# A decoder layer on one core: residual sums of the last batches on TensorE, the down product in another bank, and all orders written anew

## The chip, the cores and the metric

One core of a Trainium2 chip runs the whole kernel. The metric is device time in microseconds (us) of one execution. The core has a matrix engine (TensorE, PE in the profile, with its weight loads as PEld), a vector engine (VectorE, DVE), a scalar engine (ScalarE, ACT), GpSimd (POOL) and SyncE (SP), which here only starts transfers. Each engine runs its own list of instructions in order and waits on semaphores for the others. Matrix products land in PSUM, eight banks of 512 float32 columns by 128 partitions; everything else is in SBUF.

## The reference, cut to what matters

```python
# x: (16, 256, 128), ctx: (16, 64, 128), float32
x = _layernorm(x + attn(x))      # 16 heads of 8, linear attention, elu+1 features, own layernorm with gamma and beta
x = _layernorm(x + xattn(x, ctx))# 16 heads of 64, softmax over 64 context rows
x = _layernorm(x + ffn(x))       # I = 352
def ffn(x):                      # fp4_linear(v, w) = einsum(q(v), q(w)), q: blocks of 16 to 8 levels and back
    return fp4_linear(silu(fp4_linear(x, w_gate)) * fp4_linear(x, w_up), w_down)
```

`q` divides each block of 16 values by its largest magnitude over 6, rounds to a grid of eight magnitudes and multiplies back. All products are in float32 accuracy.

## The kernel before, in words

**Tiling.** A batch has two tiles (t = 0, 1) of 128 rows, so there are 32 tiles. Weights are folded once at the start: `m_product` (32 calls) gives, per head and half of the batches, the matrix `M` with which a tile's 16 x 64 scores come from the normed rows in two products.

**Stages of one batch.** `project_kv`, `project_q`, `kv_outer`, `kv_project`, `attn_out` (linear attention), two norms (`attn`, `post`), `x1_transpose`, then per tile `scores`, `score_max` on DVE, `scores_shift` on PE (the maxima are taken off by a product with an identity), `softmax_exp` on ACT, `fold_halves`, `score_sums`, `score_reciprocals`, `probabilities` (POOL, DVE, DVE, POOL), `p_transpose`, `keep_pT` on ACT, `cross_out`. Then `cross_residual` on DVE, `statistics` and `aggregate` on DVE, four short POOL operations for reciprocal deviation and shift, `cross_norm` on ACT, the quantisation of x2 (DVE, ACT, DVE, DVE, POOL: `x_max` to `x_dequantise`), `xf_transpose`, a split of the result into a high and a low part (`xf_cut_high` and `xf_keep_low` on DVE, `keep_xfT` on ACT), `gate_up` per tile in three float32r products for each of gate and up, `gate_tanh`, `gate_times`, `gated`, the quantisation of h (`h_max` to `h_dequantise`), `h_transpose`, `keep_hT`, `down`, `ffn_residual`, statistics, norm and the store.

**The last batch.** Batch 15 goes tile by tile from `tile_cross_out` on, through functions named `tile_...`, and its gate and up products are whole float32 products (L2912 to L2916). Both of its down products land in bank A2.

**Banks.** A1 (attention sums and small values), A2 (projections, `cross_out`, `xf_transpose`, and `down`, by `DN = A2`), S (two banks, scores), TP (two banks, TP0 and TP1: `p_transpose`, `values`, `h_transpose`), F (two banks, F0 and F1: gate and up products, then the magnitudes in the quantisation of h; batch 13 uses S for them). A product into a bank waits until the readers of what was there are done. That wait stands in the list ahead of the call.

**Orders.** The calls of a batch are not in a loop: each engine's list is written out, some 430 calls on POOL, 540 on ACT, 725 on DVE and 400 on PE, so that up to nine batches are under way at once. `keep_warm(bank, n)` issues n products of a 128 x 128 identity (each is two entries in the profile) into a bank, with no reader. It is called three times: `WARM` = 8 at the very start into A1, 7 ahead of `h_transpose(13)` and 14 ahead of `h_transpose(14)`, both into TP0.

The ends of PE's list before, waits left out: ... `p_transpose(15, 1)`, `xf_transpose(14)`, `tile_cross_out(15, 1)`, `gate_up(14, 0)`, `h_transpose(12)`, `down(12)`, `gate_up(14, 1)`, `keep_warm(TP0, 7)`, `h_transpose(13)`, `tile_xf_transpose(15, 0)`, `tile_gate_up(15, 0)`, `down(13)`, `tile_xf_transpose(15, 1)`, `tile_gate_up(15, 1)`, `keep_warm(TP0, 14)`, `h_transpose(14)`, `down(14)`, `tile_h_transpose(15, 0)`, `tile_h_transpose(15, 1)`, `tile_down(15, 0)`, `tile_down(15, 1)`.

Of the kernel before, what the change touches and what calls it, by code (L numbers as in the profile page):

```python
# [17 lines left out]
def decoder_layer(nc, x, x_t, attn_w, attn_rows, ctx_t, wq_t, wk_t, wv_t, wo_in, fw_in, out):  # L18
# [40 lines left out]
    with es:  # L59
# [57 lines left out]
        NXB, NA, NPE = 4, 5, 3  # L117
# [26 lines left out]
        fold = several("fold", 2, [P, HX * R // 2])  # L144
        ssum = several("ssum", 2, [P, HX])
        srec = several("srec", 2, [P, HX])
# [4 lines left out]
        xf_r = several("xf_r", 2, [P, 2, T * P], FP32R)  # L151
        xfT = sb("xfT", [P, T * P])
# [21 lines left out]
        DN = A2  # L174
# [5 lines left out]
        FFN_IN_S = (13,)  # L180

# [62 lines left out]
        XO_OF, GU_OF = (A2, A1), ((F0, F1), (S0, S1))  # L244

# [32 lines left out]
        WARM = 8  # L278
# [9 lines left out]
        def _(sp):  # L288
# [31 lines left out]
            load_xT(4)  # L320
            load_x(4)
            load_x(5)
            load_xT(5)
            load_xT(6)
            load_x(6)
            load_x(7)
            load_x(8)
            load_xT(7)
            load_xT(8)
            load_xT(9)  # L330
            load_x(9)
            load_x(10)
            load_x(11)
            load_xT(10)
            load_xT(11)
            load_x(12)
            store_out(0)
            store_out(1)
            load_xT(12)
            load_x(13)  # L340
            store_out(2)
            load_x(14)
            load_xT(13)
            load_xT(14)
            store_out(3)
            load_x(15)
            load_xT(15)
            store_out(4)
# [16 lines left out]
        def _(pool):  # L365
# [54 lines left out]
            def fold_halves(b, t):  # L420
                n = T * b + t
                pool.wait_ge(pe_made, n + 1)
                wait_free(pool, ssum_made, n - 1)
                p4 = pe_[n % NPE][:, :].rearrange("p (h s r) -> p h s r", h=HX, s=2)
                ge.tensor_tensor(by_head(fold[n % 2][:, :]), p4[:, :, 0, :], p4[:, :, 1, :], ALU.add).then_inc(fold_made, 1)  # L425

            def probabilities(b, t):
# [3 lines left out]
                ge.tensor_tensor(w, w, spread(srec[n % 2][:, :], HX, R), ALU.mult).then_inc(pn_made, 1)  # L431
# [83 lines left out]
            gate_up_low(0)  # L515
            gate_up_low(1)
# [4 lines left out]
            times_gamma(0)  # L521
            plus_x_beta(0)
            k_norm(1)
# [5 lines left out]
            k_norm(2)  # L529
# [6 lines left out]
            x_plus_rows(3)  # L536
            fold_halves(0, 0)
            minus_mean("post", 1)
            variance_eps("post", 1)
            k_norm(3)  # L540
            rstd_of("post", 1)
            shift_of("post", 1)
            probabilities(0, 0)
            variance_eps("attn", 2)
            fold_halves(0, 1)
# [3 lines left out]
            probabilities(0, 1)  # L549
# [3091 lines left out]
```

## Time and profile before

| what | us |
|---|---|
| median of 3 runs (372.3 to 372.66) | 372.65 |
| the profiled execution's own time | 374.35 |
| its span, first to last instruction | 372.6 |
| PE busy in the span | 351.0 |
| DVE busy | 307.9 |
| POOL busy | 269.1 |
| ACT busy | 253.4 |

The profiled execution took 1.7 us more than the median, and its span is nearly the median. PE's busy time is modelled at its ends and holds the drain of each product, so that it overstates what the array does: a 128-column float32 product is two entries of about 275 ns each, while in a row of sixteen such entries one starts every 111 ns.

### The profile page before, as it was taken

The page shows a single profiled execution, that of the slowest core. Times are in us where ns is not written, and L with a number is a line of the kernel's source. Part 1 is how long each engine was busy: PE and PEld are TensorE (multiplying, and loading weights), DVE is VectorE, ACT ScalarE, POOL GpSimd, SP SyncE. Part 2 cuts the span into 40 slices and gives each one's busy share as a digit, 9 for nine tenths or more (in the row PEclk, how much of TensorE's full clock was granted, in tenths as well). Part 3 has the DMA queues.
Part 4 walks back from the last instruction along what each step waited for, and adds up shares of the span by engine and source line. Part 5 has one row for each costly group of instructions (what it writes and reads, how often), then busy time and mean ns, then how long its engine had stood idle before and what let it go on. Part 6 is the DMA issues. An engine that isn't in the chain of part 4 may idle for free.

```text
span 372.6 us, 7321 instructions
## 1 busy us (share of the span) xinstructions
PE 351.0 (94%) x2143; PEld 268.7 (72%) x2143; DVE 307.9 (83%) x858; ACT 253.4 (68%) x533; POOL 269.1 (72%) x453
## 2 busy tenths in 40 slices
PE   7999998999998999999999999999999999998874
PEld 6688655775775968778678867786777788887663
DVE  2798756658689998869989779979998998999994
ACT  2757867586677678668687767868767656864553
POOL 4403549967988689969779895898989569784535
PEclk9999999999999999999999999999999999999998
DMA  7900100001000001000000000000000000000010
GB/s 251 300 2 16 30 1 14 16 16 29 15 17 14 2 15 43 16 30 17 15 29 14 17 1 17 28 3 0 17 15 2 15 2 0 8 23 14 3 30 28
DMA packets 13586, 10.44 MB, mean 28 GB/s; under 512 B 971, under 2 KB 12396, under 8 KB 13548
## 3 DMA queue, kind: packets, MB, share of 16 engines
q1 hardware_dynamic: 12540, 7.89, 7.0%
q10 hardware_dynamic: 1008, 2.10, 1.7%
q8 instruction: 18, 0.29, 0.3%
q14 instruction: 20, 0.16, 0.1%
HBM read 7.88 MB, written 2.10 MB: 27 GB/s over the span
## 4 chain that ended last, share of the span: by engine, by line
PE 71%; POOL 8%; DVE 8%; issue 6%; ACT 5%; DMA 1%; POOLq 0%; ACTq 0%; DVEq 0%
PE A L2860 13%; PE S L2833 12%; PE TP L2823 7%; PE F L2879 6%; PE TP L2851 6%; PE A L2895 5%; PE A L2784 3%; PE S L2842 3%; PE TP L2762 2%; POOL pe L431 2%; PE S L2762 2%; PE F L2762 2%; PE TP L2888 2%; PE A L2797 2%; DMA wqkT<-in_wk_t 1%
## 5 line engine op out<-in xcount | busy, mean ns | idle before, releaser
L431 POOL TENSOR_TENSOR pe<-pe,srec 128x1024 f32<-128x1024 f32 x32 | 60.9, 1904 | 9.2 <-DVE srec L1835 8.9
L2833 PE MATMUL S<-M,x1T 128*128 128x512 f32 x128 | 60.7, 597 | 1.5 <-ACT pe L1064 1.4
L2860 PEld LDWEIGHTS A<-wvoT,wqkT 128*128 128x128 f32 x480 | 56.4, 192 | 3.1 <-issue 1.8
L2860 PE MATMUL A<-wvoT,wqkT 128*128 128x128 f32 x480 | 58.0, 276 | 0.1
L425 POOL TENSOR_TENSOR fold<-pe 128x512 f32<-128x512 f32 x32 | 40.8, 1276 | 14.5 <-ACT pe L1064 14.2
L1818 DVE TENSOR_REDUCE smax<-S 128x16 fp32r<-128x1024 f32 x32 | 38.7, 1210 | 3.2 <-PE S L2833 3.1
L1064 ACT ACTIVATE pe<-S 128x1024 f32<-128x1024 f32 x32 | 32.6, 1020 | 10.6 <-PE S L2842 10.3
L1069 ACT ACTIVATE wqkT<-TP 128x1024 f32<-128x1024 f32 x32 | 32.6, 1019 | 4.3 <-PE TP L2851 4.1
L2833 PEld LDWEIGHTS S<-M,x1T 128*128 128x128 f32 x128 | 22.2, 190 | 18.3 <-issue 15.3
L2879 PE MATMUL F<-w_gu_r,xf_r 128*128 128x352 f32 x168 | 35.0, 344 | 0.1
L2851 PE MATMUL TP<-ident,pe 128*128 128x128 f32 x256 | 33.5, 274 | 1.6 <-POOL pe L431 1.0
L2851 PEld LDWEIGHTS TP<-ident,pe 128*128 128x128 f32 x256 | 28.8, 140 | 6.2 <-issue 3.1
L2823 PE MATMUL TP<-HW,ctx_f 128*64 128x512 f32 x128 | 31.0, 605 | 0.0
L2879 PEld LDWEIGHTS F<-w_gu_r,xf_r 128*128 128x128 f32 x168 | 26.9, 188 | 4.4 <-issue 3.2
L2895 PEld LDWEIGHTS A<-w_dn,hT 128*128 128x128 f32 x180 | 21.5, 192 | 6.6 <-issue 4.7
L441 POOL TENSOR_TENSOR hv<-hv,ham 128x704 f32<-128x704 f32 x15 | 20.8, 1389 | 6.0 <-DVE hv L1910 5.8
L1829 DVE TENSOR_REDUCE ssum<-fold 128x16 f32<-128x512 f32 x32 | 21.7, 677 | 4.2 <-POOL fold L425 4.2
L416 POOL TENSOR_TENSOR kn<-fk,ky 128x256 f32<-128x256 f32 x16 | 10.1, 632 | 20.7 <-DVE ky L1790 20.6
L2895 PE MATMUL A<-w_dn,hT 128*128 128x128 f32 x180 | 23.0, 277 | 2.0 <-ACT hT L1089 2.0
L2842 PE MATMUL S<-smax,ident_r 128*128 128x512 f32 x64 | 21.8, 422 | 1.7 <-DVE smax L1818 1.7
L409 POOL TENSOR_TENSOR xb<-x_sb,rows 128x512 f32<-128x512 f32 x16 | 20.4, 1275 | 3.9 <-DMA rows<-in_attn_rows 2.7
L1058 ACT ACTIVATE wvoT<-TP 128x1024 f32<-128x1024 f32 x16 | 16.3, 1022 | 6.8 <-PE TP L2823 6.8
(247 smaller groups left out, 890.2 us busy)
## 6 DMA issues: line engine op xcount, KB each, us to landing
xT<-in_x_t SPq DMA_DIRECT2D x16, 128.0 KB, 2.1
x_sb<-in_x SPq DMA_DIRECT2D x16, 128.0 KB, 2.1
out<-yf SPq DMA_DIRECT2D x15, 128.0 KB, 1.8
M<-in_fw SPq DMA_DIRECT2D x1, 560.0 KB, 11.0
wqkT<-in_wq_t ACTq DMA_DIRECT2D x2, 256.0 KB, 4.5
wqkT<-in_wk_t ACTq DMA_DIRECT2D x2, 256.0 KB, 5.8
ctx_f<-in_ctx_t ACTq DMA_DIRECT2D x2, 256.0 KB, 6.9
wvoT<-in_wv_t ACTq DMA_DIRECT2D x1, 512.0 KB, 9.2
```

The lines of the kernel that those rows point to most:

```text
L425: ge.tensor_tensor(by_head(fold[n % 2][:, :]), p4[:, :, 0, :], p4[:, :, 1, :], ALU.add).then_inc(fold_made, 1)
L431: ge.tensor_tensor(w, w, spread(srec[n % 2][:, :], HX, R), ALU.mult).then_inc(pn_made, 1)
L1064: sc.activation(pe_[n % NPE][:, :], S[:, :], ACT.Exp, scale=SCALE).then_inc(pe_made, 1)
L1069: sc.activation(pT[n % 2], TP[:, :].rearrange("p (a n) -> p a n", a=NJ), ACT.Copy).then_inc(pT_kept, 1)
L1818: ve.tensor_reduce(smax[n % 2][:, :], by_head(S[:, :]), AX.X, ALU.max, negate=True).then_inc(smax_made, 1)
L2823: last = te.matmul(TP[par * R:par * R + R, half * BANK:half * BANK + BANK], ctx_f[:, b * R:b * R + R], HW[:, par, 4 * half:4 * half + 4, : ...
L2833: last = te.matmul(S[:, half * BANK:half * BANK + BANK], x1T[b % 2][:, t * P:t * P + P], M[:, b // BH, HC * half:HC * half + HC, b % BH * ...
L2842: last = te.matmul(S[:, half * BANK:half * BANK + BANK], ident_r[:, :], spread(smax[n % 2][:, HC * half:HC * half + HC], HC, R), start=Fal ...
L2851: last = te.transpose(TP[:, j * P:j * P + P], pe_[n % NPE][:, j * P:j * P + P], ident[:, :])
L2860: last = te.matmul(A2[:, t * P:t * P + P], pT[n % 2][:, j, :], vo[b % 2][:, j, :], start=(j == 0), stop=(j == NJ - 1))
L2879: last = te.matmul(bk[:, 0:I], part(xf_r[b % 2][:, left, :], t), w_gu_r[:, right, m, :], start=(n == 0), stop=(n == len(PARTS) - 1))
L2895: last = te.matmul(DN[:, t * P:t * P + P], hT[b % 2][:, t, k * P:k * P + P], w_dn[:, k, :], start=(k == 0), stop=(k == NK - 1))
```

## The change

- Batches 13 and 14: `cross_out` and `down` begin each tile's sum with a product of the identity and the residual (`x1`, `x2`), so that `cross_residual` and `ffn_residual` fall away on DVE; `statistics` and the norm read PSUM. The same for the down product of both tiles of batch 15.
- Batches 12, 13 and 14: `gate_up` makes whole float32 products (two per tile in place of six in float32r). `xf_cut_high` and `xf_keep_low` fall away on DVE, and `keep_xfT` copies from PSUM.
- `down` lands in TP0 (`DN = TP0`). The down product of batch 15's second tile lands in A1, the first one's stays in A2.
- `xf_r` lies in the space of `GT`, `xfT` gets two buffers. `NFO` = 2 only names a number that was there.
- `WARM` goes from 8 to 13, and there are now five calls of `keep_warm`: at the start (13), 3 into F0 ahead of `m_product(0, 0)`, 7 into TP0 ahead of `h_transpose(13)`, 4 into F0 ahead of `tile_gate_up(15, 0)`, 15 into TP0 ahead of `tile_h_transpose(15, 0)`.
- The lists of all five engines are written anew from the first batch to the last.

```diff
-        WARM = 8
+        WARM = 13
-        DN = A2
+        DN = TP0
+        WHOLE_GATE = (12, 13, 14)
+
+        SUM_ON_PE = (13, 14)
+
+        TILE_SUM_ON_PE = True
...
+        DN_OF = (A2, A1) if TILE_SUM_ON_PE else (A2, A2)
...
+                y = part(A2, t) if b in SUM_ON_PE else yx[b % 2][:, t, :]
+                norm("cross", b, t, x2[b % 3][:, NBX * t:NBX * t + NBX, 0:BLK], blocks(y, NBX))
...
             def keep_xfT(b):
-                act.wait_ge(xf_cut_made, b + 1)
-                sc.activation(xf_r[b % 2][:, 0, :], xf_cut[:, :], ACT.Copy).then_inc(xfT_kept, 1)
+                if b in WHOLE_GATE:
+                    act.wait_ge(xfT_made, b + 1)
+                    sc.activation(xfT[b % 2][:, :], A2[:, 0:T * P], ACT.Copy).then_inc(xfT_kept, 1)
...
+                if b in SUM_ON_PE:
+                    pe.wait_ge(x1_made, T * b + T)
+                    te.matmul(part(A2, t), ident[:, :], x1[b % NA][:, t, :], start=True, stop=False)
                 for j in range(NJ):
...
+                if b in WHOLE_GATE:
+                    for m, bk in enumerate(ffn_banks(b)):
+                        last = te.matmul(bk[:, 0:I], part(xfT[b % 2], t), w_gu[:, m, :], start=True, stop=True)
+                    last.then_inc(gu_made, 1)
+                    return
...
             def down(b):
                 pe.wait_ge(hT_kept, b + 1)
                 for t in range(T):
+                    if b in SUM_ON_PE:
+                        pe.wait_ge(x2_made, T * b + T)
+                        te.matmul(blocks(part(DN, t), NBX), ident[:, :], x2[b % 3][:, NBX * t:NBX * t + NBX, 0:BLK],
+                                  start=True, stop=False)
```

The end of PE's list:

```diff
+            pe.wait_ge(hg4_made, 13)
+            gate_up(14, 0)
             pe.wait_ge(xg_made, 15)
             tile_cross_out(15, 1)
...
             pe.wait_ge(h_made, 29)
             gate_up(14, 1)
-            pe.wait_ge(hT_kept, 13)
+            pe.wait_ge(pT_kept, 32)
             keep_warm(TP0, 7)
             h_transpose(13)
...
+            pe.wait_ge(hT_kept, 14)
+            down(13)
+            pe.wait_ge(xfT_kept, 15)
             tile_xf_transpose(15, 0)
-            pe.wait_ge(h_made, 30)
+            pe.wait_ge(hg4_made, 15)
+            keep_warm(F0, 4)
             tile_gate_up(15, 0)
             pe.wait_ge(xfT_kept, 16)
-            down(13)
-            pe.wait_ge(yf_made, 14)
             tile_xf_transpose(15, 1)
+            pe.wait_ge(normed["ffn"], 28)
+            h_transpose(14)
             pe.wait_ge(hg4_made, 14)
             tile_gate_up(15, 1)
-            pe.wait_ge(hT_kept, 14)
-            keep_warm(TP0, 14)
-            h_transpose(14)
+            pe.wait_ge(hT_kept, 15)
+            down(14)
+            pe.wait_ge(normed["ffn"], 30)
+            keep_warm(TP0, 15)
+            tile_h_transpose(15, 0)
+            pe.wait_ge(normed["ffn"], 30)
+            tile_h_transpose(15, 1)
             pe.wait_ge(xfT_kept, 17)
```

`normed["ffn"]` reaches 30 when ACT has done `ffn_norm(14, 1)`; `hg4_made` reaches 15 when DVE has done `h_rounded(14)`.

On the other engines the lists now end so:

- DVE, after `tile_cross_residual(15, 1)`: `gate_times(14, 1)`, `tile_x_reciprocal(15, 0)`, `gated(14, 1)`, `tile_x_scaled(15, 0)`, `h_max(14)`, `h_reciprocal(14)`, `h_scaled(14)`, `tile_statistics("cross", 15, 1)`, `tile_x_rounded_up(15, 0)`, `tile_x_rounded(15, 0)`, `tile_aggregate("cross", 15, 1)`, `h_rounded_up(14)`, `statistics("ffn", 13)`, `aggregate("ffn", 13)`, `h_rounded(14)`, the five steps of the quantisation of x2 for (15, 1), `tile_gate_times(15, 0)`, `tile_gated(15, 0)`, `tile_h_max(15, 0)`, `tile_h_reciprocal(15, 0)`, `tile_h_scaled(15, 0)`, `tile_gate_times(15, 1)`, `tile_h_rounded_up(15, 0)`, `tile_gated(15, 1)`, `statistics("ffn", 14)`, `tile_h_max(15, 1)`, `aggregate("ffn", 14)`, `tile_h_reciprocal(15, 1)`, `tile_h_scaled(15, 1)`, `tile_h_rounded(15, 0)`, `tile_h_rounded_up(15, 1)`, `tile_h_rounded(15, 1)`, then statistics and aggregates of both last tiles.
- ACT: ..., `keep_hT(14)`, `tile_gate_tanh(15, 1)`, `tile_h_magnitudes(15, 0)`, `tile_h_magnitudes(15, 1)`, `ffn_norm(14, 0)`, `ffn_norm(14, 1)`, `tile_keep_hT(15, 0)`, `tile_keep_hT(15, 1)`, `tile_ffn_norm(15, 0)`, `tile_ffn_norm(15, 1)`. Before, `ffn_norm(14, 0)` and `(14, 1)` stood behind both `tile_keep_hT`.
- POOL: ..., four short operations for `"ffn", 14`, `tile_h_dequantise(15, 0)`, `tile_h_dequantise(15, 1)`, the short operations of the last two norms.

## Rows read from the trace of the kernel before

**Rows 1.** Stretches: us, busy time of PE, PEld, DVE, ACT, POOL, granted clock, DMA.
```profile
0.00:10.00 10.00, 7.21 (x36) 6.54 (x37) 3.27 (x15) 2.12 (x3) 4.56 (x24) 1.00 0.80 253
...
50.00:60.00 10.00, 8.32 (x36) 4.98 (x33) 7.17 (x22) 5.91 (x17) 6.91 (x13) 1.00 0.05 14
60.00:300.00 240.00, 234.55 (x1442) 176.74 (x1442) 202.93 (x585) 175.90 (x369) 198.12 (x312) 1.00 0.05 16
...
320.00:344.40 24.40, 22.54 (x155) 19.26 (x154) 23.34 (x58) 15.72 (x29) 15.47 (x25) 1.00 0.06 17
344.40:364.50 20.10, 16.19 (x115) 13.86 (x114) 19.10 (x52) 10.06 (x21) 8.95 (x21) 1.00 0.05 15
```
**Rows 2.** The chain that ended last, a piece: start, us on the chain, what.
```profile
284.48 1.34 PE A L2895 x12
285.81 1.72 PE S L2833 x4
287.75 0.97 PE F L2879 x6
288.72 0.87 PE TP L2851 x8
290.03 1.78 PE A L2860 x16
```
**Rows 3.** The page's costliest groups: busy us, mean ns, idle before.
```profile
L1818 DVE TENSOR_REDUCE smax<-S 128x16 fp32r<-128x1024 f32 x32 | 38.7, 1210 | 3.2 <-PE S L2833 3.1
...
L1064 ACT ACTIVATE pe<-S 128x1024 f32<-128x1024 f32 x32 | 32.6, 1020 | 10.6 <-PE S L2842 10.3
```
**Rows 4.** Two lines of DVE: ns min/median/max, first and last start.
```profile
L1915 DVE TENSOR_TENSOR yf<-A,x x15: 392/425/426, 134.8 to 364.7; 128x256 f32<-128x256 f32 x15
...
L1876 DVE TENSOR_TENSOR xf_r<-A,xf_cut x15: 390/418/426, 103.3 to 343.0; 128x256 fp32r<-128x256 f32 x15
```
**Rows 5.** PE in order of time, the start: start, us, operation.
```profile
1.45 3.78 PE L2934 MATMUL A<-fold 128*128 128x128 f32 x16 [1.45 <-POOL fold L371]
6.57 2.08 PE L2742 MATMUL F<-wqkT 64*128 64x128 f32 x16 [1.34 <-DMA wqkT<-in_wk_t]
...
11.00 1.16 PE L2742 MATMUL TP<-wqkT 64*128 64x128 f32 x16
...
12.97 1.65 PE L2762 MATMUL F<-ctx_r,GT 128*128 128x512 f32 x6
...
16.08 1.66 PE L2762 MATMUL TP<-ctx_r,GT 128*128 128x512 f32 x6
```
**Rows 6.** All engines in order of time, the start.
```profile
14.74 1.28 DVE L1712 TENSOR_TENSOR GT<-TP,pe 128x512 fp32r<-128x512 f32 x2
```
**Rows 7.** PE in order of time, `scores(15, 0)` and `tile_cross_out(15, 1)`.
```profile
319.95 1.88 PE L2833 MATMUL S<-M,x1T 128*128 128x512 f32 x4
...
341.74 2.02 PE L2905 MATMUL A<-wvoT,wqkT 128*128 128x128 f32 x16 [0.49 <-ACT wqkT L1069]
```
**Rows 8.** All engines in order of time, the end: the filler products and their surroundings.
```profile
357.88 3.29 PE L2934 MATMUL TP<-ident 128*128 128x128 f32 x28
...
359.54 0.88 ACT L1036 ACTIVATE yf<-yf,shift_ffn,rstd_ffn 128x128 f32<-128x128 f32 x2 [1.00 <-POOL shift_ffn L462]
...
361.25 0.64 PEld L2888 LDWEIGHTS TP<-ident,hv 128*128 128x128 f32 x6 [0.28 <-POOL hv L441]
```
**Rows 9.** The same view, from the last rounding of h to the last residual sum.
```profile
363.93 0.53 DVE L1997 SCALAR_TENSOR_TENSOR hv<-S,hv 128x352 f32<-128x352 f32 x1
...
364.54 0.79 POOL L508 TENSOR_TENSOR hv<-hv,ham 128x352 f32<-128x352 f32 x1 [0.40 <-DVE hv L1997]
...
365.47 0.52 PE L2922 MATMUL TP<-ident,hv 128*128 128x128 f32 x3 [0.44 <-POOL hv L508]
...
367.04 0.94 PE L2928 MATMUL A<-w_dn,hT 128*128 128x128 f32 x6 [0.38 <-DVE yf L2003]
...
368.01 0.29 DVE L2003 TENSOR_TENSOR yf<-A,x 128x128 f32<-128x128 f32 x1 [0.48 <-PE A L2928]
```

More of the change, by code:

```diff
@@ L2527, in _ @@
+            xf_cut_high(10)
+            gated(9, 1)
+            xf_keep_low(10)
+            h_max(9)
+            h_reciprocal(9)
+            h_scaled(9)
+            score_sums(13, 0)
+            keep_kvT(14)
+            score_reciprocals(13, 0)
+            h_rounded_up(9)
+            ffn_residual(8)
+            h_rounded(9)
+            statistics("ffn", 8)
+            x_max(11)
+            aggregate("ffn", 8)
+            score_max(13, 1)
             attn_residual(14)
             statistics("attn", 14)
+            x_reciprocal(11)
@@ L3165, in _ @@
             scores(4, 1)
+            cross_out(3, 1)
+            pe.wait_ge(ya_made, 6)
+            kv_project(6)
+            pe.wait_ge(pT_kept, 8)
+            values(5)
+            pe.wait_ge(kvo_kept, 7)
+            kv_outer(7)
+            pe.wait_ge(yx_made, 4)
+            project_q(6)
+            pe.wait_ge(vo_kept, 6)
+            p_transpose(4, 0)
+            scores_shift(4, 1)
+            pe.wait_ge(fq_made, 7)
+            xf_transpose(1)
+            pe.wait_ge(kvT_kept, 8)
@@ L3279, in _ @@
             project_q(9)
+            pe.wait_ge(pe_made, 15)
+            scores(7, 1)
+            pe.wait_ge(xg_made, 6)
+            kv_project(9)
+            pe.wait_ge(vo_kept, 9)
+            h_transpose(3)
+            attn_out(9)
+            pe.wait_ge(fq_made, 10)
+            xf_transpose(4)
+            scores_shift(7, 1)
+            pe.wait_ge(hT_kept, 4)
+            down(3)
+            pe.wait_ge(hg4_made, 4)
+            gate_up(4, 0)
+            pe.wait_ge(xf_low_made, 5)
@@ L3280, in _ @@
+            xf_transpose(5)
+            pe.wait_ge(ya_made, 10)
+            kv_outer(10)
             pe.wait_ge(pe_made, 16)
             x1_transpose(8)
[L3282 to L3287 removed]
+            pe.wait_ge(yf_made, 4)
+            p_transpose(7, 0)
+            pe.wait_ge(xf_low_made, 6)
+            project_kv(12)
             pe.wait_ge(x1T_kept, 9)
@@ L3526, in _ @@
             pe.wait_ge(vo_kept, 16)
-            p_transpose(14, 0)
+            h_transpose(11)
             pe.wait_ge(x1T_kept, 16)
             scores(15, 0)
+            pe.wait_ge(h_made, 25)
+            gate_up(12, 1)
+            pe.wait_ge(hT_kept, 12)
+            down(11)
+            scores_shift(15, 0)
+            pe.wait_ge(xfT_kept, 13)
+            xf_transpose(13)
+            pe.wait_ge(yf_made, 12)
+            p_transpose(14, 0)
+            pe.wait_ge(pe_made, 31)
+            scores(15, 1)
```

2943 lines of the change are left out of this document (1445 added, 1498 removed).

## The prediction

> **What bounds the kernel now.** I read the stretches first, then the chain that ended last, then the timeline of both ends. Up to 300 us PE sets the pace: 234.6 us busy of 240 between 60 and 300, with DVE at 202.9 [rows 1]. A large part of that busy time is drain. What each stage costs when PE is fed is read from the chain [rows 2]: `down` 1.34 us, `scores` 1.72, `gate_up` 0.97 (six float32r entries of 352 columns), `p_transpose` 0.87, `cross_out` 1.78. From their columns the others follow: `h_transpose` (six transposes of eight) 0.65, `xf_transpose` (two) 0.22, `project_q` (256 float32 columns) 0.43, `kv_project` (128) 0.22, `m_product` (three float32r entries of 512) 0.70, a scores shift (two) 0.43. From 320 us on the picture turns: PE has gaps, and DVE is busy 23.3 us of 24.4 and then 19.1 of 20.1 up to the last rounding at 364.5 [rows 1]. Behind that comes a chain in which every engine waits for one other: rounding, POOL product, transpose, copy, down product, residual sum, norm [rows 9]. So the same microsecond is worth most on PE in the middle, on DVE from 320 to 364, and on any link of the chain at the end.
>
> I count from three marks. `scores(15, 0)` starts at 319.95, and `tile_cross_out(15, 1)` ends at 341.74 + 2.02 = 343.76 [rows 7]. The last rounding ends at 363.93 + 0.53 = 364.46 [rows 9]. The span ends at 372.6.
>
> **Part 1, the start: -1.3 us.** PE's first sixteen entries take 2.08 us where the same product takes 1.16 us a little later [rows 5]: the array runs at half its rate until about 11 us. Eight warm-up products end at 5.2 us, and PE is idle to 6.57, where the load of `wk` lands. Thirteen take 13/8 of 3.78 = 6.1 us at that rate and would end at 7.6, a microsecond past that landing; if the rate doubles while they run, they end near 7. Either way `g_product(0)` ends between 7.8 and 8.9 in place of 8.65. What m-products wait for is DVE's cutting of G, done at 14.74 + 1.28 = 16.0 [rows 6], upon which PE goes on at 16.08 [rows 5]; it moves by -0.8 to +0.3, and I take -0.4. The three fillers ahead of `m_product(0, 0)` (0.7 us) lie in the slack before that mark and cost nothing; without that slack they would cost 0.7. Second, between `m_product(0, 2)` and `scores(0, 0)`, where PE has no gap, the new list holds 0.9 us less: `m_product(1, 15)` (0.70) and `project_q(2)` (0.43) now stand behind it and `kv_project(2)` (0.22) before it. They fall into the stretch 50 to 60, which has 1.7 us of idle PE [rows 1]. Together -1.3, bounds -2.2 and +0.6.
>
> The Trainium skill ("TensorE: Matmul & The Clock Gate", Part 1, the HAM clock gate) says that half rate is the default state and that activity releases it. The trace agrees in the durations, though the granted clock of the first 10 us reads 1.00 [rows 1]. By that rule an unbroken row of warm-ups brings the release forward, the -0.8 end; by the row alone the thirteen only delay the first product, the +0.3 end.
>
> **Part 2, from there to `scores(15, 0)`: +0.6 us.** The calls ahead of that mark differ by `h_transpose(11)` (0.65), `xf_transpose(12)` (0.22) and `gate_up(12, 0)`, which are there now, and `p_transpose(14, 0)` (0.87), which no longer is. A float32 product of 352 columns costs 1.72 / 2 x 352 / 512 = 0.59 us by the scores [rows 2], so a whole `gate_up` is 1.18 in place of 0.97. Two identity products in `cross_out(13)` cost 1.78 / 8 = 0.22 each. Sum: 0.65 + 0.22 + 1.18 - 0.87 + 0.44 = +1.6. Against it stands how well the lists cover PE's waits. Between `scores` and its shift DVE needs 1.21 us [rows 3] and, as I allow, 0.24 of handing over; between the shift and the next product into S, ACT needs 1.02 [rows 3] and 0.2 again. I summed PE's work between the two calls in both lists. Before, 7 of 32 shifts are covered too little, by 3.2 us together, and 6 of the successors by 2.6; now 6 by 2.0 and 4 by 0.6. That is 3.2 us in favour. With `down` in TP0, a bank that must first be copied out, waits of about 0.9 us behind `down` and 2.0 more between `h_transpose` and the next user of TP come in, and A2 loses its own (0.2). Other covers about cancel. I take -1.0 of the -3.2 to +2.5 that these leave open, because both effects are only partly on PE's path. The new lists of DVE, ACT and POOL may move as much, which I cannot weigh and which is in these bounds. So +0.6, bounds -2.5 and +3.5.
>
> **Part 3, from `scores(15, 0)` to the end of `tile_cross_out(15, 1)`: +2.2 us.** Before it is 23.8 us. Now the list in between is: `scores`, `gate_up(12, 1)`, `down(11)`, shift, `xf_transpose(13)`, `p_transpose(14, 0)`, `scores`, `p_transpose(14, 1)`, `cross_out(14, 0)`, shift, `cross_out(14, 1)`, `p_transpose(15, 0)`, `gate_up(13, 0)`, `h_transpose(12)`, `gate_up(13, 1)`, `tile_cross_out(15, 0)`, `down(12)`, `xf_transpose(14)`, `p_transpose(15, 1)`, `gate_up(14, 0)`, `tile_cross_out(15, 1)`. At the costs above this is 23.9 us of work without a wait. Waits that I cannot cover: `h_transpose(12)` for POOL, whose list does `probabilities(15, 0)` and a fold first, 0.3; `gate_up(13, 1)` for `gated(13, 0)`, the same banks S, 0.8; `tile_cross_out(15, 0)` for `cross_norm(14, 1)`, which now reads A2 itself and before had a copy in SBUF, some 0.4; `p_transpose(15, 1)` for `ffn_residual(12)`, the reader of TP0, 0.5; small handings over. That gives 26.0. Bounds 24.5 and 27.
>
> **Part 4, to the last rounding: -1.4 us.** Before it is 20.7 us, filled by DVE [rows 1]. Behind `tile_cross_residual(15, 1)` DVE had 21.7 us of work by summed durations (52 entries that overlap a little, so 19.1 busy [rows 1]); by the same durations the new list has 16.4. Of the change itself, `ffn_residual(13)` (0.42 [rows 4]) and `xf_keep_low(14)` are gone here (all together the change takes about 4.7 us off DVE: two `cross_residual`, two `ffn_residual`, six cuts and lows at 0.42 each [rows 4], two tile sums at 0.29 [rows 9], less of it in this stretch); the rest was done earlier. But the gain is not 5.3 us, since a chain takes DVE's place. `tile_gate_up(15, 0)` waits for `h_rounded(14)` (F0 is read by it), and behind this wait stand four fillers: 0.9 us, then the product 1.2, tanh 0.5, while DVE has 1.5 us of other work. Adding link by link with before's durations I get the last rounding 19.3 us after `tile_cross_out(15, 1)`. Bounds 18 and 20.5.
>
> **Part 5, the end chain: +2.5 us.** This is the step I trust most. PE now runs `down(14)`, waits for `ffn_norm(14, 1)`, then does 15 fillers and only then `tile_h_transpose(15, 0)`. ACT does that norm behind `tile_h_magnitudes(15, 1)`, so it ends 0.5 (its kin's duration) + 0.9 [rows 8] = 1.4 us after `tile_h_scaled(15, 1)`. The transposes could start by their own data, POOL's product after the rounding (0.79 [rows 9]), 1.3 and 2.5 us after the same instruction. The fillers are 28 entries in 3.29 us before [rows 8], of which 0.16 is drain: 0.224 a product, 3.4 us for 15. Hence the first transpose comes at +4.8 and the second at +5.2 in place of +1.4 and +2.6. Before, 14 fillers stood ahead of a transpose whose wait (361.25, for POOL [rows 8]) came right at their end: the bank was free early and they cost nothing. Now the bank is free late. The second transpose starts 3.6 us after the last rounding ends in place of 1.0: +2.6. The identity product adds 0.22 to the last `tile_down`, the residual sum on DVE (0.29 and a handing over of 0.04 [rows 9]) goes. Together +2.5, bounds +1.5 and +3.
>
> "PSUM — Partial Sum Buffer" of the Trainium skill (Engine vs sequencer instructions) says that matrix products start and complete in program order and only weight loads are pulled ahead. By that rule the transposes cannot slip past the fillers; if they could, this part would be about -0.1.
>
> **Sum.** -1.3 + 0.6 + 2.2 - 1.4 + 2.5 = +2.6 us on the span of 372.6. The profiled execution took 374.35, 1.7 over the median; I add the difference to the median: 372.65 + 2.6 = 375.2.
>
> **Rivals.**
> (a) The new lists win in the middle, faster in the end. Place: the shifts and scores of batches 1 to 15. If the 3.2 us of short covers on S come off PE's path in full, the waits on TP0 are hidden behind other work, and the start gives its 2.2, parts 1 and 2 are -2.2 - 1.6 = -3.8 in place of -0.7. From a part 1 plus 2 under -3.3 the whole is faster. With part 3 at its good half too (+1.2) the time is 372.65 - 3.8 + 1.2 - 1.4 + 2.5 = 371.2. For it: PE sets the pace there, and idle is only a few us. Against it: PE's added work is certain. Chance 0.28.
> (b) The fillers do not hold the end up: if `ffn_norm(14, 1)` were early, they would fit in the 3.7 us that I find between `down(14)` and the transposes. Then part 5 is -0.1 and the time 372.6. ACT's list speaks against it. Chance 0.12.
> (c) TP0 is the worse bank: all the TP waits are on the path (+3.5 in part 2), 378. For it: TP already has four users a batch, each with a copy of about 1 us behind it. Chance 0.1.
> The forecast itself has the other 0.5, within 373.6 to 376.8.
>
> **Chances.** A change under 0.2% (0.75 us) can't be told from none in this kernel. Slower holds the forecast, (c), and little of the others: 0.61. Faster is (a) less its edge and some of (b): 0.26. Same: 0.13. The range reaches into (a) and (c): 371.2 to 377.5.
>
> **What would show it.** Right: a row of 30 filler entries on PE that begins right behind `ffn_norm(14, 1)` and ends ahead of `tile_h_transpose(15, 0)` with POOL's product long done; eight filler entries behind `h_rounded(14)`; the last rounding near 365 to 366; early entries of PE at the short duration before 11 us; DVE some 4.7 us less busy. Wrong: `scores(15, 0)` starting earlier than 317, which is (a); or no idle time of PE's data at those fillers, which is (b).

## The result, and the profile after

| what | before | after |
|---|---|---|
| median of 4 runs each | 372.65 (372.3 to 372.77) | 378.17 (377.63 to 378.68) |
| the profiled execution's own time | 374.35 | 377.71 |
| its span | 372.6 | 375.9 |
| `scores(0, 0)` starts | 51.72 | 49.53 |
| `scores(15, 0)` starts | 319.95 | 318.07 |
| `tile_cross_out(15, 1)` ends | 343.76 | 344.54 |
| the last rounding ends | 364.46 | 363.58 |

The ratio is 1.0149 with the interval 1.0129 to 1.0169: slower, and by 5.5 us where 2.6 were forecast. The executions of before lie in two groups, which the experiments bring out: 84 later ones give 35 between 372.1 and 373.0 and 49 between 373.3 and 374.9. The four beside the changed kernel were all of the lower group, the profiled one of the upper; against the medians of the three later studies (373.77, 373.48 and 373.63) the changed kernel is 4.4 to 4.7 us slower.

The four marks show where the time went. The start gained 2.2 us, the stretch to `scores(15, 0)` gave 0.3 back, the next gave 2.7 back, DVE's stretch gained 1.7, and the end from the last rounding grew from 8.1 to 12.3 us. This is PE in order of time over that end, to be read against [rows 8, 9] (start, us, operation; xN is the number of entries in a row; in brackets the idle time ahead and what ended it):

```profile
359.26 0.83 PE L2927 MATMUL TP<-w_dn,hT 128*128 128x128 f32 x6
...
363.52 5.00 PE L2971 MATMUL TP<-ident 128*128 128x128 f32 x30 [3.43 <-ACT yf L1045]
...
368.36 0.82 PE L2954 MATMUL TP<-ident,hv 128*128 128x128 f32 x6
...
370.67 0.83 PE L2964 MATMUL A<-w_dn,hT 128*128 128x128 f32 x6
```

`down(14)` is done at 360.1. Then PE stands idle for 3.43 us until `ffn_norm(14, 1)` has read TP0, issues the thirty filler entries, and only then comes to the transposes of batch 15. Those had their data long before, as the same stretch on the other engines shows:

```profile
362.66 0.81 ACT L1045 ACTIVATE yf<-TP,shift_ffn,rstd_ffn 128x128 f32<-128x128 f32 x2 [0.19 <-POOL shift_ffn L471]
...
363.06 0.52 DVE L2028 SCALAR_TENSOR_TENSOR hv<-S,hv 128x352 f32<-128x352 f32 x1
...
363.66 0.79 POOL L517 TENSOR_TENSOR hv<-hv,ham 128x352 f32<-128x352 f32 x1 [0.36 <-DVE hv L2028]
```

POOL's product of the second tile ends at 364.45. The transposes start at 368.36, almost 4 us later. Before, the second transpose started 0.1 us behind that product [rows 9].

The row takes 5.00 us where I had worked out 3.4 for it. The stretches say why (start and end; length; busy us of PE, PEld, DVE, ACT, POOL; granted clock; DMA share and rate):

```profile
363.00:364.00 1.00, 0.48 (x2) 0.48 (x3) 0.55 (x2) 0.47 (x2) 0.64 (x2) 0.52 0.00 0
364.00:365.00 1.00, 1.00 (x7) 1.00 (x7) 0.00 (x0) 0.00 (x0) 0.45 (x1) 0.50 0.44 131
...
366.00:367.00 1.00, 1.00 (x9) 1.00 (x8) 0.00 (x0) 0.00 (x0) 0.00 (x0) 0.77 0.00 0
367.00:368.00 1.00, 1.00 (x11) 1.00 (x10) 0.00 (x0) 0.00 (x0) 0.00 (x0) 1.00 0.00 0
```

The granted clock is half, the lower of TensorE's two levels (1.2 of 2.4 GHz), from 363 until within the slice from 366. The number of entries in a microsecond, 7 against 11, shows it a second time. The fillers lie behind the idle time that they were there to bridge.

The start in the same view, against [rows 5]. The thirteen warm-up products end at 6.1 us, 0.2 before the load of `wk`, and the product behind them runs at 1.16 us in place of 2.08:

```profile
1.45 4.68 PE L2971 MATMUL A<-fold 128*128 128x128 f32 x26 [1.45 <-POOL fold L380]
6.36 1.16 PE L2762 MATMUL F<-wqkT 64*128 64x128 f32 x16 [0.23 <-DMA wqkT<-in_wk_t]
```

The stretches that answer to [rows 1]:

```profile
60.00:300.00 240.00, 237.66 (x1479) 180.22 (x1478) 209.29 (x590) 175.66 (x366) 202.55 (x317) 1.00 0.05 16
...
344.50:363.60 19.10, 12.55 (x82) 9.75 (x80) 16.39 (x44) 8.04 (x19) 7.57 (x17) 0.99 0.05 15
```

PE has less idle time in the middle (2.3 us in place of 5.4) and 37 entries more. In the last stretch DVE is no longer full, with 16.4 us of 19.1 in place of 19.1 of 20.1.

### The profile page after: what moved, and what is told of

The parts are those of the page before. It is cut to its first block, busy times and chain, and to the rows that moved or that the text cites. A ratio compares the mean times of both kernels' runs of the same rounds, so it can differ in the third digit from the quotient of the medians.

```text
span 375.9 us, 7382 instructions
## 1 busy us (share of the span) xinstructions
PE 355.8 (95%) x2177; PEld 271.3 (72%) x2177; DVE 309.1 (82%) x846; ACT 253.4 (67%) x533; POOL 270.3 (72%) x453
## 4 chain that ended last, share of the span: by engine, by line
PE 42%; POOL 26%; issue 21%; DVE 4%; ACT 3%; DMA 2%; POOLq 1%; ACTq 0%; DVEq 0%
PE A L2883 8%; PE S L2853 7%; POOL pe L440 5%; PE TP L2871 4%; PE TP L2843 4%; PE F L2907 4%; POOL fold L434 3%; POOL hv L450 2%; PE TP L2927 2%; PE F L2782 2%; DMA wqkT<-in_wk_t 2%; POOL x L477 2%; PE A L2804 2%; PE S L2862 2%; POOL xb L418 1%
## 5 line engine op out<-in xcount | busy, mean ns | idle before, releaser
L2907 PE MATMUL F<-w_gu_r,GT 128*128 128x352 f32 x144 | 30.5, 347 | 0.2 <-DVE h L1911 0.2
L2907 PEld LDWEIGHTS F<-w_gu_r,GT 128*128 128x128 f32 x144 | 23.2, 189 | 6.3 <-issue 4.4
L2927 PE MATMUL TP<-w_dn,hT 128*128 128x128 f32 x180 | 23.3, 277 | 0.4 <-ACT hT L1105 0.4
L2927 PEld LDWEIGHTS TP<-w_dn,hT 128*128 128x128 f32 x180 | 21.6, 192 | 2.0 <-ACT hT L1105 1.5
L425 POOL TENSOR_TENSOR kn<-fk,ky 128x256 f32<-128x256 f32 x16 | 11.1, 696 | 15.5 <-DVE ky L1810 15.5
L1070 ACT ACTIVATE wvoT<-TP 128x1024 f32<-128x1024 f32 x16 | 16.4, 1025 | 7.9 <-PE TP L2843 7.8
```

What stands on the lines that cost most here:

```text
L2907: last = te.matmul(bk[:, 0:I], part(xf_r[b % 2][:, left, :], t), w_gu_r[:, right, m, :], start=(n == 0), stop=(n == len(PARTS) - 1))
L2927: last = te.matmul(part(DN, t), hT[b % 2][:, t, k * P:k * P + P], w_dn[:, k, :], start=(k == 0 and b not in SUM_ON_PE), stop=(k == NK - 1))
```

## The experiments

"Fillers" are the products of `keep_warm`. Times are medians with all runs' range. The experiments ran in three sets, each on another chip: `a_15_early`, `a_no_15`, `b0_before_again` and `b_warm_13`; `a_fill_early` and the three `b13_` kernels; `a_15_twice` and the three `a_fe_` kernels. The kernel before ran beside each set on the same chip (medians 373.77, 373.48 and 373.63), and the ratios are to it. The changed kernel wasn't run again, so every difference to its 378.17 reaches across sets, and so do those between kernels of two of them.

| kernel | us | ratio to before, interval | span |
|---|---|---|---|
| changed kernel | 378.17 (377.63 to 378.68) | 1.0149, 1.0129 to 1.0169 | 375.9 |
| `a_15_early` | 373.55 (373.18 to 373.95) | 1.0009, 0.9993 to 1.0024 | 371.5 |
| `a_no_15` | 375.52 (374.94 to 375.6) | 1.0059, 1.0037 to 1.0082 | 373.7 |
| `a_15_twice` | 377.0 (376.9 to 377.34) | 1.0092, 1.0066 to 1.0118 | 375.5 |
| `a_fill_early` | 372.93 (372.44 to 373.54) | 0.9988, 0.9973 to 1.0003 | 370.7 |
| `a_fe_nosum` | 373.85 (373.39 to 375.1) | 1.0013, 0.9998 to 1.0027 | 373.3 |
| `a_fe_w8` | 373.77 (372.65 to 374.73) | 1.0008, 0.9992 to 1.0025 | 371.7 |
| `a_fe_nowhole` | 376.8 (375.71 to 378.89) | 1.0089, 1.0058 to 1.012 | 375.0 |
| `b0_before_again` | 373.66 (372.4 to 374.32) | 1.0015, 0.9995 to 1.0035 | 372.5 |
| `b_warm_13` | 372.73 (372.22 to 373.17) | 0.9976, 0.9955 to 0.9996 | 371.4 |
| `b13_tilesum` | 372.6 (372.23 to 372.98) | 0.9975, 0.996 to 0.999 | 370.6 |
| `b13_whole` | 373.45 (373.18 to 373.88) | 1.0008, 0.9994 to 1.0022 | 371.7 |
| `b13_whole_tilesum` | 373.33 (372.86 to 373.79) | 1.0001, 0.9987 to 1.0015 | 371.1 |

The four marks of the result divide the profiled execution of each kernel into five stretches (us):

| kernel | to `scores(0, 0)` | to `scores(15, 0)` | to the end of `tile_cross_out(15, 1)` | to the last rounding | to the end |
|---|---|---|---|---|---|
| before | 51.72 | 268.23 | 23.81 | 20.70 | 8.14 |
| `b0_before_again` | 51.65 | 268.23 | 23.79 | 20.70 | 8.13 |
| `b_warm_13` | 50.50 | 268.27 | 23.81 | 20.70 | 8.12 |
| `b13_tilesum` | 49.91 | 268.22 | 23.81 | 20.70 | 7.96 |
| `b13_whole` | 50.02 | 268.33 | 24.35 | 20.83 | 8.17 |
| `b13_whole_tilesum` | 49.60 | 268.33 | 24.35 | 20.83 | 7.99 |
| changed kernel | 49.53 | 268.54 | 26.47 | 19.04 | 12.32 |
| `a_15_early` | 49.70 | 268.52 | 26.48 | 19.04 | 7.76 |
| `a_no_15` | 49.87 | 268.61 | 26.47 | 19.04 | 9.71 |
| `a_15_twice` | 50.46 | 268.58 | 26.47 | 19.04 | 10.95 |
| `a_fill_early` | 49.58 | 268.59 | 26.47 | 18.31 | 7.75 |
| `a_fe_w8` | 50.73 | 268.44 | 26.48 | 18.28 | 7.77 |
| `a_fe_nosum` | 49.87 | 268.40 | 26.40 | 20.89 | 7.74 |
| `a_fe_nowhole` | 49.70 | 271.20 | 27.36 | 19.03 | 7.71 |

Where two kernels have the same lists in a stretch, it has the same length within 0.2 us. Only the first stretch differs between executions of equal lists: with thirteen warm-ups it is 49.5 to 50.5. So a part's worth is best read from its own stretch.

### The fifteen fillers: moved, dropped, doubled

The first moves them ahead of the wait, into bank A1, which is free by then. The second drops them. The third has them in both places.

```diff
 a_15_early            down(14)
+            pe.wait_ge(xg_made, 17)
+            keep_warm(A1, 15)
             pe.wait_ge(normed["ffn"], 30)
-            keep_warm(TP0, 15)
             tile_h_transpose(15, 0)
 a_no_15: only the "-" line      a_15_twice: only the "+" lines
```

> The changed kernel; only the 15 filler products ahead of tile_h_transpose(15, 0) go into A1, ahead of the wait for ffn_norm(14, 1), behind the wait for xg_made 17. Theory 1 (the late fillers hold up the end chain, and run at half rate because PE was idle 3.4 us before): the second last-batch transpose starts near 364.6 in place of 368.6, span 371.9, median 378.2 - 4.1 = 374.1. Rival 2 (the middle and the end's DVE work are the loss, the fillers are hidden): within 0.7 us of 378.2.

> The changed kernel without the 15 filler products. Theory 1: the transposes start at 363.5 and 364.6, but PE was idle from 360.0, the granted clock falls to half near 363 and the 6 transposes and 16 entries of the down products run at half rate: about 1.5 us lost of the 4.1 won, median 375.6. If the fillers are worth nothing at all: 374.1, as with early fillers. Rival 2: 378.2.

> The changed kernel with 15 fillers into A1 ahead of the wait for ffn_norm(14, 1) and the 15 late ones kept behind it: 30 products in all. It parts the two reasons for the end chain's loss. Theory 1a (the late row costs its length at full rate, 3.4 us, and in the changed kernel another 1.6 because PE's idle time ahead of it had let the granted clock fall to half): here PE is busy before, the clock stays at 1.00 and the row takes 3.4, so 373.55 + 3.4 = 376.9. Theory 1b (the rate has nothing to do with the idle time): the row takes 5.0 as in the changed kernel, 378.2 or more.

Moving them gives 4.6 us back (378.17 to 373.55; 374.1 was expected). PE in order of time shows the row at the full rate, in the place of the idle time, and the transposes behind their own data again, the second at 364.75:

```profile
360.09 3.51 PE L2971 MATMUL A<-ident 128*128 128x128 f32 x30
363.69 0.55 PE L2954 MATMUL TP<-ident,hv 128*128 128x128 f32 x3
364.75 0.52 PE L2954 MATMUL TP<-ident,hv 128*128 128x128 f32 x3 [0.52 <-POOL hv L517]
```

Without them it is 375.52, 2.0 us worse than with early ones and 2.65 better than with late ones. The same idle time stands there, and the whole chain behind it runs at the lower level, a half-rate transpose (0.90 against 0.55) and down product (1.49 against 0.83):

```profile
363.94 0.90 PE L2954 MATMUL TP<-ident,hv 128*128 128x128 f32 x3 [3.44 <-ACT yf L1045]
...
366.10 1.49 PE L2964 MATMUL A<-w_dn,hT 128*128 128x128 f32 x6
```

So the fillers are worth 2.0 us where nothing waits behind them. With both rows the late one has no idle time ahead and runs at the full rate:

```profile
360.90 3.51 PE L2971 MATMUL A<-ident 128*128 128x128 f32 x30
364.50 3.62 PE L2971 MATMUL TP<-ident 128*128 128x128 f32 x30
```

That kernel takes 377.0, as the first theory of its expectation has it (376.9) and not the second (378.2). The 4.6 us are thus split, by medians into 3.45 (377.0 less 373.55) and 1.2 (378.17 less 377.0). The stretch behind the last rounding, which leaves the start out, gives 3.2 (10.95 less 7.76) and 1.4 (12.32 less 10.95). The first is the row that the transposes must wait out, which I had forecast. The second is the half rate that the idle time had brought on, which I had not.

### The four fillers as well

```diff
 a_fill_early (a_15_early, and:)
+            keep_warm(TP1, 4)
             pe.wait_ge(hg4_made, 15)
-            keep_warm(F0, 4)
             tile_gate_up(15, 0)
```

> The changed kernel with both late filler rows moved: 15 into A1 ahead of the wait for ffn_norm(14, 1), and the 4 ahead of tile_gate_up(15, 0) into TP1 ahead of the wait for h_rounded(14). Theory 1 (a filler row behind the last wait delays what follows by its own length): tile_gate_up(15, 0) starts 0.9 us earlier and the end follows, 373.55 - 0.9 = 372.6. Rival 3 (DVE's work ahead of tile_gate_times(15, 0) covers the four): 373.5.

372.93, 0.6 us less than `a_15_early`, where 0.9 were expected: the ranges overlap in part, the direction is right. In the traces the stretch to the last rounding is 0.7 shorter (18.31 in place of 19.04), and the others are unchanged. With all fillers ahead of their waits the changed kernel stands at 0.9988 of before, with 1 inside the interval. Its last rounding ends at 362.95 and its span 7.75 us later.

### What the start is worth

```diff
 b_warm_13 (before)                a_fe_w8 (a_fill_early)
-        WARM = 8                  -        WARM = 13
+        WARM = 13                 +        WARM = 8
```

`b0_before_again` is the kernel before, word for word, as the measure of what "no change" looks like.

> The kernel before, unchanged. Question: the changed kernel's span is 3.3 us longer than that of before (375.9 against 372.6), its median 5.5 us. Theory A: the one profiled execution of before was 1.7 us slower than its usual ones (374.35 against 372.65), for instance by the start, so its usual span is near 370.9. Theory B: profiling adds 1.7 us outside the span. A expects spans near 370.9 to 371 in most executions and one entry of about 372.65; B expects spans of 372.6 with times near 374.4.

> The kernel before with 13 warm-up products in place of 8, nothing else. In the profile of the changed kernel the rate doubles near 4.3 us and g_product(0) takes 1.16 us in place of 2.08. Theory S (the usual execution of before is cold up to 11 us as its profile shows): 1 to 1.7 us faster than before, 371 to 371.6. Theory N (the usual execution of before is warm early and only the profiled one was cold): within 0.4 us of 372.65, slower if anything.

> The changed kernel with early fillers and 8 warm-ups in place of 13. On the lists of before 13 warm-ups gave 1.0 us in the median and took away the executions of 373.6 to 374.8. Theory: the same here, median 373.9 with a spread of 2 us. Rival (the start's new lists wait for other things): 372.9.

The unchanged kernel came out at 1.0015 of itself, over ten executions in the same two groups (372.4 to 372.6 and 373.6 to 374.3). In every execution the time is 1.7 to 1.9 us over the span, as in the profiled ones. So theory B has nothing for it, and theory A holds for the lower group alone: spans of 370.6 to 370.9 there, of 371.8 to 372.5 in the upper, with seven of the ten. Thirteen warm-ups alone bring before to 372.73, 0.9976 (0.9955 to 0.9996), and no execution lies above 373.17: they remove the upper group. By its number this is theory N; against the kernel before beside it (373.77) it is the gain of 1.0 us that theory S asked for. Each theory took the executions of before to be of one kind. Taking the five added warm-ups out of `a_fill_early` costs 0.8 us and brings the upper group back (up to 374.73). PE's first rows of the kernel with 13 and, below, of the one with 8:

```profile
1.45 5.92 PE L2934 MATMUL A<-fold 128*128 128x128 f32 x26 [1.45 <-POOL fold L371]
7.29 1.29 PE L2742 MATMUL F<-wqkT 64*128 64x128 f32 x16
```

```profile
1.45 3.78 PE L2971 MATMUL A<-fold 128*128 128x128 f32 x16 [1.45 <-POOL fold L380]
6.15 2.08 PE L2762 MATMUL F<-wqkT 64*128 64x128 f32 x16 [0.92 <-DMA wqkT<-in_wk_t]
```

With eight, the first product takes 2.08 us and rows stay slow to about 10 us; with thirteen it takes 1.29. `scores(0, 0)` starts at 50.50 in place of 51.72 in these two executions, and in the changed kernel at 49.53. How much of the 2.2 us between 51.72 and 49.53 is the warm-ups and how much the rearranged list can't be told. With thirteen warm-ups the first stretch varies by 1 us between executions: four with the list of before have 49.6 to 50.5, seven with the new one 49.5 to 50.5, and the row of warm-ups itself takes 4.6 to 5.9 us. The list is thus worth 0.2 us between the means of these (50.0 and 49.8), and 1.0 between the three executions with eight (51.7 and 50.7). No profile of an execution of the lower group with eight was taken, so that its start went at the higher rate is an inference: from what thirteen warm-ups do, and from every later stretch being the same in all profiles of equal lists.

### Whole gate products and residual sums, one at a time

From before with 13 warm-ups. `b13_whole` makes the gate products of batches 12 to 14 whole and drops the six cuts and lows from DVE's list, which stays as it was otherwise. `b13_tilesum` starts the two down products of batch 15 with the identity product, the second one in A1, and drops the two residual sums. The third has both.

```diff
 b13_whole
+        WHOLE_GATE = (12, 13, 14)
-            xf_cut_high(12)
-            xf_keep_low(12)
...
-            pe.wait_ge(xf_low_made, 13)
+            pe.wait_ge(xfT_kept, 13)
 b13_tilesum
+        DN_OF = (A2, A1)
...
+                te.matmul(blocks(part(DN_OF[t], t), NBX), ident[:, :], x2[...], start=True, stop=False)
-            tile_ffn_residual(15, 0)
-            tile_ffn_residual(15, 1)
-            pe.wait_ge(yf_made, 16)
+            pe.wait_ge(xg_made, 17)
             tile_down(15, 1)
```

> The kernel before with 13 warm-ups and one part of the change: batches 12 to 14 with whole float32 gate and up products, orders otherwise kept. DVE loses six entries of 0.42, PE gains 6 x 0.21. Theory (DVE bounds 320 to 364): 1 to 2 us faster than 372.73, 371.2. Rival (PE's longer products and copies in the same waits): within 0.4 of 372.7.

> The kernel before with 13 warm-ups and one part of the change: the residual of batch 15's two tiles as an identity product in tile_down, the second tile's down product in A1. The residual sum (0.29 and 0.04 of handing over) leaves the end chain, the second product no longer waits for the first tile's residual sum (0.4), the identity product adds 0.22 once or twice: theory, 0.3 to 0.5 us faster than with 13 warm-ups alone, 372.3. Rival (identity products on the path eat it): 372.7.

> Both parts together on the lists of before, with 13 warm-ups: if they add up, 372.73 - 1.5 - 0.4 = 370.8. This would be a version under both kernels.

The whole products were to bring 1 to 2 us, and cost 0.7: 373.33 against 372.6 between the two kernels with residual sums on PE, on one chip, with ranges that overlap by 0.1, and 373.45 against 372.73 between those without. In my prediction DVE sets the pace from 320 us, so that 2.5 us less of it should have told. It didn't. Between 320 and 364 (columns as above), the kernel with whole products, then the one without:

```profile
320.00:364.00 44.00, 38.64 (x254) 31.39 (x252) 40.07 (x98) 24.00 (x48) 23.27 (x41) 1.00 0.06 16
```

```profile
320.00:364.00 44.00, 38.08 (x267) 32.84 (x265) 41.67 (x105) 24.86 (x50) 23.85 (x43) 1.00 0.06 16
```

DVE is 1.6 us less busy and PE 0.6 more. All six cuts and lows lie in the stretch from `scores(15, 0)` to `tile_cross_out(15, 1)` (326.6 to 342.3 in `b_warm_13`), and in both pairs this stretch takes 24.35 in place of 23.81 us, while DVE's idle time in it grows from 1.1 to 2.3 us: what DVE gave free it spent waiting. So in this stretch DVE was not the bound. The stretch behind it, up to the last rounding, held none of the six; it is 0.13 longer, and whether DVE bounds it this run doesn't test.

The residual sums of batch 15 on PE take the wait of 0.38 us ahead of the second down product out [rows 9]. This is the last rounding and that product, in `b_warm_13` and, below, in `b13_tilesum`:

```profile
362.75 0.53 DVE L1997 SCALAR_TENSOR_TENSOR hv<-S,hv 128x352 f32<-128x352 f32 x1
...
365.86 0.94 PE L2928 MATMUL A<-w_dn,hT 128*128 128x128 f32 x6 [0.38 <-DVE yf L2003]
```

```profile
362.11 0.53 DVE L2003 SCALAR_TENSOR_TENSOR hv<-S,hv 128x352 f32<-128x352 f32 x1
...
364.90 0.39 PE L2932 MATMUL A<-x,ident 128*128 128x128 f32 x2
365.12 0.83 PE L2935 MATMUL A<-w_dn,hT 128*128 128x128 f32 x6
```

The product starts 0.7 us sooner, but 0.6 of that is the earlier start of the whole execution. Counted from the last rounding it starts 0.1 sooner (2.48 us behind its end in place of 2.58), and the end stretch is 0.16 shorter (7.96 in place of 8.12), where 0.3 to 0.5 were expected. The median of 372.6 is the lowest of all and beats before (0.9975, 0.996 to 0.999), but by medians it can't be told from `b_warm_13` at 372.73. With both parts it is 373.33 where 370.8 was expected: the two effects do add up, but the larger one has the other sign.

### The same two parts, taken out of the changed kernel

From `a_fill_early`. `a_fe_nosum` puts the residual sums of 13 and 14 back on DVE, with their waits. `a_fe_nowhole` puts the cuts back, at three places of the new list that I chose.

```diff
 a_fe_nosum                          a_fe_nowhole
-        SUM_ON_PE = (13, 14)        -        WHOLE_GATE = (12, 13, 14)
+        SUM_ON_PE = ()              +        WHOLE_GATE = ()
+            cross_residual(13)      +            xf_cut_high(12)
             statistics("cross", 13) +            xf_keep_low(12)
...                                               statistics("ffn", 10)
+            ffn_residual(14)        ...
             statistics("ffn", 14)
```

> The changed kernel with early fillers and batches 13 and 14 with residual sums on DVE again (the last batch's sums stay on PE). PE loses eight identity products of 0.22, DVE gains four entries of 0.42, and A2 and TP0 come free after the residual sum and not only after the norm. Theory R (holding the bank until ACT's norm costs more than DVE's 0.42): 0.3 to 1 us faster, 372.3. Rival (DVE sets the end's pace): 0.5 to 1.5 us slower, 373.9.

> The changed kernel with early fillers (372.93) and batches 12 to 14 back to split operands and float32r gate and up products, cuts put into DVE's list near their transposes. On the lists of before the whole products cost 0.7 us. Theory W (they cost on these lists too): 372.9 - 0.5 = 372.4. Rival (these lists are made for them, DVE has no room at those places): 373.3 to 374.

Without the sums it is 373.85, 0.9 us slower: on these lists the identity products of 13 and 14 do earn that. My first theory had them at -0.6, the wrong sign; the rival was right. How they earn it is less clear. The profiled execution, at 375.1 the slowest of twelve, shows the lower rate from 356 on, behind idle stretches of 0.61, 0.86 and 0.91 us on PE (stretches as above, and the gate product in order of time, to be read against 1.35 us for the same four entries in the changed kernel):

```profile
355.00:356.00 1.00, 0.12 (x1) 0.00 (x0) 0.66 (x3) 0.96 (x3) 0.89 (x2) 1.00 0.00 0
356.00:357.00 1.00, 0.97 (x5) 1.00 (x6) 0.93 (x3) 0.28 (x2) 0.00 (x0) 0.53 0.05 14
```

```profile
357.53 2.31 PE L2951 MATMUL S<-w_gu,xfT 128*128 128x352 f32 x4
```

This is not the usual case: only one other execution is like it (375.09, with the same mean granted clock of 0.995), and the other ten read 0.998 to 1.0 and have a median of 373.77, still 0.8 us over `a_fill_early`. So the fallen rate explains about 0.1 of the 0.9 us. Whether the rest is DVE's four more instructions isn't shown, since no execution of the usual kind was profiled.

`a_fe_nowhole` came out at 376.8, which neither theory has (372.4 and 373.3 to 374). PE in order of time shows a wait of my making, for the low part of batch 12, and the products behind it at the lower rate. The stretch to `scores(15, 0)` is 2.6 us longer by it:

```profile
318.45 1.21 PE L2913 MATMUL F<-w_gu_r,GT 128*128 128x352 f32 x6 [3.31 <-DVE GT L1903]
...
320.90 2.61 PE L2859 MATMUL S<-M,x1T 128*128 128x512 f32 x3
```

Three score products take 2.61 us there, where four take 1.88 at the full rate [rows 7]. The new lists have no room for the cuts at that place, so this run says nothing of what the whole products are worth on them. It is inconclusive, except that it repeats the pattern of the end: idle for 3.3 us, then half rate.

## Why the prediction was wrong, step by step

The direction was right, and so was the cause; the size was not, 378.17 against 375.2 and outside the range (371.2 to 377.5). Of the 3.0 us between them part 5 makes 1.7, the reference 1.7, and parts 1 to 4 together -1.0; another 0.5 is that the changed kernel's median lies over its profiled execution (378.17 against 377.71).

**Part 5, the end chain: +4.2 us in place of +2.5. This term was mis-sized.** The mechanism is as forecast: thirty entries right behind `ffn_norm(14, 1)`, POOL's product long done, the transposes behind the row; `a_15_early` and `a_15_twice` show it. The step "The fillers are 28 entries in 3.29 us before [rows 8] ... 3.4 us for 15" failed. It took the duration from a row that ran without idle time ahead. Here PE had 3.43 us of idle time ahead of the row, and the row took 5.00, at half rate for most of it; without its last 0.16 of drain that is 4.84 against 3.4, or 1.4 of the 1.7 us that this part is off. I had put those 3.7 us into my own working, under rival (b), and didn't ask what they would do to the clock, although the start of the same trace shows both rates [rows 5].

The row is in the stretches of the result: a granted clock of 0.50 behind 3.43 us of idle time, and the same behind 3.44 us in `a_no_15`; in `a_15_twice`, without the idle time, it stayed at 1.00. The Trainium skill ("TensorE: Matmul & The Clock Gate", Part 1, the HAM clock gate) gives the low clock as the default state and as that of an engine which has been idle. The runs agree, by the figures just given. I had used that section for the start and not for the end.

**The reference: 1.7 us under the profile's own time.** "The profiled execution took 374.35, 1.7 over the median; I add the difference to the median." The three runs shown were all of the lower group, while the profile, from which every term came, was of the upper. The later runs show that it was no outlier: 49 of 84 executions of before are of the upper group. Sum and reference belonged to different groups: the new kernel starts with 13 warm-ups and has lost the slow start, so most of the gain of part 1 exists only against the upper group. Added to 374.35, the sum gives 377.0, 1.2 us from what was measured. The median of before over the later runs, some 373.6, lies between.

**Part 1, the start: -2.2 us in place of -1.3**, at the end of my bounds. The early end was right: warm-ups without a break bring the full rate forward, and the product behind them takes 1.16 us in place of 2.08. That the rearranged list gives the 0.9 which I had counted isn't shown: by the profiles it is somewhere between 0.2 and 1.0. That the three fillers ahead of `m_product(0, 0)` cost nothing wasn't tried by itself.

**Part 2, to `scores(15, 0)`: +0.3 in place of +0.6.** This leg is 268.5 us in place of 268.2. From 60 to 300 PE's busy time grew by 3.1 us and its idle time fell by as much, which fits added work taken up by better covers; the two weren't parted. That `down` in TP0 is the worse bank, rival (c), has nothing for it in this leg; the bank alone wasn't tried.

**Part 3, to the end of `tile_cross_out(15, 1)`: +2.7 in place of +2.2.** 26.5 us against the 26.0 worked out call by call. The total was right in part by luck, since two errors cancel. PE was busy for 25.5 us, the drain ahead of each idle stretch included, where I had counted 23.9 of work, and idle for 1.0, where I had counted 2.1 of waits. Of the four waits named, the ones for `h_transpose(12)` and `gate_up(13, 1)` are there (0.26 and 0.57), the other two leave no idle time, and one of 0.17 ahead of `xf_transpose(14)` wasn't named.

**Part 4, to the last rounding: -1.7 in place of -1.4.** 19.0 against 19.3. The sum of the chain held, and DVE had idle time in this stretch as forecast. The eight entries behind `h_rounded(14)` are there, after 1.2 us of idle time, and `a_fill_early` values them at 0.6 us.

**DVE's busy time: 309.1 in place of 307.9, not 4.7 less.** Twelve instructions went (846 in place of 858), and the durations of all groups of DVE add up to 351.2 in place of 354.5 us, 3.3 less. Busy time counts overlapping entries once: it was 46.6 us under that sum before and is 42.1 under it now. So DVE's instructions overlap less than before, and its busy time rose by 1.2 us while its work fell.

**What bounds the kernel from 320 us.** I had written that a microsecond is worth most "on DVE from 320 to 364". `b13_whole` shows otherwise up to 343: three cuts and three lows less in DVE's list gave nothing there. Of the rest, up to 364, no run takes DVE's work out by itself. In the forecast this did no harm, since parts 3 and 4 were summed over PE and over the chain.

**The rivals.** (a) needed parts 1 and 2 under -3.3; they gave -1.9. (b) was not so: PE waited 3.43 us for ACT's norm, as argued. (c) named a time of 378 for a reason that isn't in the trace; that its number fits is chance. The account as a whole, by medians: 378.17; 4.6 for the fifteen fillers moved, 0.6 for the four, which leaves 372.93. Before with 13 warm-ups is at 372.73. So all the rest of the change together, the sums, the whole products, the bank and five new lists, comes to 0.2 us, which is nothing that medians can tell. The stretches agree, and show that it is a balance and not nothing. Against `b_warm_13`, `a_fill_early` needs 0.3 more to `scores(15, 0)` and 2.7 more to the end of `tile_cross_out(15, 1)`. It then needs 2.4 less to the last rounding and 0.4 less behind it. This fits the work that the new lists do earlier, but it wasn't parted by runs. Within this the sums of batches 13 and 14 are worth 0.9. Which part gives that back stays open: the whole products cost 0.7 on the old lists, on the new ones their cost isn't isolated.

## What to carry to other kernels

Filler products belong ahead of the last wait, in a bank that is already free. Behind it, they come after the clock has fallen, and what follows must wait until they are done: here the same fifteen products were worth -2.0 us in one place and +2.65 in the other. When a step puts idle time on PE, price what follows it at the lower rate. Before adding a sum to a median, see whether the profiled execution and the median belong to the same group of runs, and take both from the same one. And compare stretches between marks, not clock times: a shift from the start is in every later time.

## What the runs showed of the hardware

- **Half rate behind idle time.** After 3.4 us of idle PE the granted clock read 0.50 (changed kernel, `a_no_15`); after 3.3 us it read 1.00 for the first slice behind it and then 0.50 (`a_fe_nowhole`). It isn't a matter of one long stretch alone: in one execution of `a_fe_nosum` it fell behind two of 0.9 us, 1.45 us of products between them; ten of the twelve executions of that kernel read a mean clock of 0.998 or more.
- **The way back differs.** In the changed kernel the full rate came back within the row of fillers, after some 3 us. In `a_no_15`, where only transposes, down products and idle time follow, the clock stayed low to the end of PE's work:

```profile
366.00:367.00 1.00, 1.00 (x7) 1.00 (x7) 0.00 (x0) 0.41 (x1) 0.00 (x0) 0.50 0.06 8
...
369.00:370.00 1.00, 0.29 (x2) 0.00 (x0) 0.48 (x2) 0.00 (x0) 0.13 (x2) 0.50 0.00 0
```

- **Eight warm-up products, two groups of executions.** Their means lie 1.3 to 1.7 us apart, on each of the three chips of the experiments; with thirteen only the lower group is left (22 executions of `b_warm_13` and `b13_tilesum`, none over 373.2). In all profiles with thirteen the row of warm-ups takes 4.6 to 5.9 us, and `scores(0, 0)` starts at 49.5 to 50.5.
- **The granted clock of the first 10 us reads 1.00 while the products take their long duration.** At the start the durations are what is to be read.
